# Score products on 64-column quarters of the TensorE array in a decoder layer

## The reference

```
x = layernorm(x + gelu(x @ (w1 @ w2.T * sparse_mask) + b2))
x = layernorm(x + cross_attention(x, ctx, wq, wk, wv, wo))   # 32 query heads, 8 key/value heads of 128, 64 context rows, rope
x = layernorm(x + x @ W.T + b + routed_lora(x))              # router softmax over 8 experts, rank 16
```

```
scores = jnp.einsum('bhqd,bhkd->bhqk', q, k) / scale
attn = jax.nn.softmax(scores + m[:, None, :, :], axis=-1)
out = jnp.einsum('bhqk,bhkd->bhqd', attn, v)
return out.transpose(0, 2, 1, 3).reshape(bs, sq, HQ * DV) @ wo
```

## Time and profile before

| | |
|---|---|
| median of 3 runs | 532.72 us (531.84 to 533.61) |
| profiled execution | 532.04 us, span 530.2 us, granted TensorE clock 0.994 |
| TensorE matmul busy | 507.9 us, 3149 records |
| score products (L350) | 1024 records, 32 blocks |
| VectorE, ScalarE, GpSimd busy | 408.9, 259.8, 269.0 us |

### The profile page before, as it was taken

The page is one execution under the profiler, slowest core; times in us unless marked ns, Lnnn a source line. Parts: engine busy times, 40 slices in busy tenths (PEclk is TensorE's granted clock), DMA queues, the critical chain, the costliest instruction groups (busy, mean ns, idle before and its releaser), DMA issues.

```text
span 530.2 us, 9033 instructions
## 1 busy us (share of the span) xinstructions
PE 507.9 (96%) x3149; PEld 419.4 (79%) x3149; DVE 408.9 (77%) x742; ACT 259.8 (49%) x462; POOL 269.0 (51%) x343
## 2 busy tenths in 40 slices
PE   5899999999999999999999999999999999969992
PEld 4677788888888888888888888888888888758781
DVE  3556888878878877787788788878887888999575
ACT  4372375753555355636563555354546544263332
POOL 2173255944575367527653854484547533136624
PEclk9999999999999999999999999999999999999997
DMA  8942010203020302020212023002200230000004
GB/s 302 356 129 90 1 41 0 77 4 121 0 81 0 119 0 79 22 96 0 79 56 63 0 79 108 11 0 79 79 0 5 76 61 1 2 0 1 1 2 158
DMA packets 27598, 31.51 MB, mean 59 GB/s; under 512 B 6321, under 2 KB 14769, under 8 KB 27578
## 3 DMA queue, kind: packets, MB, share of 16 engines
q1 hardware_dynamic: 27578, 31.25, 18.2%
HBM read 29.15 MB, written 2.10 MB: 59 GB/s over the span
## 4 chain that ended last, share of the span: by engine, by line
PE 90%; DVE 3%; DMA 2%; POOL 1%; SPq 1%; issue 1%; ACT 1%; DVEq 0%; POOLq 0%; ACTq 0%
PE bank L255 25%; PE bank L257 24%; PE bank L256 24%; PE bank L350 11%; PE bank L357 3%; PE bank L261 2%; DMA CTX<-in_ctx_dram 2%; DVE VWl L1105 1%; PE bank L300 1%; DVE BST L1155 1%; DVE X L1347 1%; PE bank L390 0%; PE bank L301 0%; ACT VWh L768 0%; SPq L203 0%
## 5 line engine op out<-in xcount | busy, mean ns | idle before, releaser
L1694 POOL TENSOR_TENSOR QS<-QS,SIN 128x512 f32<-128x512 f32 x64 | 82.7, 1292 | 98.9 <-ACT QS L768 93.7
L1105 DVE TENSOR_TENSOR VWl<-bank,VWh 64x512 fp32r<-64x512 f32 (+1 forms) x132 | 90.8, 688 | 20.3 <-ACT VWh L768 18.3
L255 PE MATMUL bank<-XTh,WQh 128*128 128x512 f32 x256 | 101.6, 397 | 0.0
L257 PE MATMUL bank<-XTh,WQl 128*128 128x512 f32 x256 | 99.9, 390 | 0.0
L256 PE MATMUL bank<-XTl,WQh 128*128 128x512 f32 x256 | 99.9, 390 | 0.0
L768 ACT ACTIVATE QS<-bank 128x512 f32<-128x512 f32 x64 | 38.3, 598 | 116.6 <-PE bank L257 116.3
L768 ACT ACTIVATE VWh<-bank 64x512 fp32r<-64x512 f32 (+1 forms) x132 | 78.2, 593 | 27.4 <-PE bank L257 24.2
L350 PEld LDWEIGHTS bank<-KK,QR 64*128 64x128 f32 x1024 | 59.6, 188 | 10.9 <-issue 10.8
L1219 DVE TENSOR_TENSOR bank<-bank,COS 128x512 f32<-128x512 f32 x64 | 44.6, 697 | 30.0 <-ACT QS L768 29.3
L350 PE MATMUL bank<-KK,QR 64*128 64x64 f32 x1024 | 64.1, 275 | 0.0
L1700 POOL TENSOR_TENSOR SM<-SM,RI 128x512 f32<-128x512 f32 x32 | 33.4, 1045 | 53.9 <-DVE RI L1265 53.8
(11 more groups left out here) (145 smaller groups left out, 955.8 us busy)
## 6 DMA issues: line engine op xcount, KB each, us to landing
WQr<-in_L_xattn_wq_dram SPq DMA_DIRECT2D x8, 1024.0 KB, 5.5
WOr<-in_L_xattn_wo_dram SPq DMA_DIRECT2D x8, 1024.0 KB, 5.5
KVr<-in_L_xattn_wk_dram SPq DMA_DIRECT2D x8, 256.0 KB, 5.3
KVr<-in_L_xattn_wv_dram SPq DMA_DIRECT2D x8, 256.0 KB, 5.6
out_dram<-X SPq DMA_DIRECT2D x8, 256.0 KB, 2.1
X<-in_x_dram SPq DMA_DIRECT2D x3, 512.0 KB, 10.0
WQr<-in_L_attn_w_dram SPq DMA_DIRECT2D x4, 256.0 KB, 3.1
WOr<-in_L_attn_w_dram SPq DMA_DIRECT2D x4, 256.0 KB, 4.9
```

Source lines behind the costliest of these rows:

```text
L255: pe.matmul(o, lh, rh, start=start, stop=False)
L257: return pe.matmul(o, ll, rh, start=False, stop=stop)
L1105: return dve.tensor_tensor(o, i, f32(hi), ALU.subtract)
L1694: pool.tensor_tensor(q, q, SIN[:, :].unsqueeze(1).broadcast_to([P, 2, S]), ALU.mult)\
```

## The change

Each score product of 64 rows by 128 tokens becomes two of 64 rows by 64 tokens. The first 64 tokens of a tile use columns 0 to 63 of the array and write bank partitions 0 to 63, the second 64 tokens columns 64 to 127 and partitions 64 to 127. With the two heads on the two row halves this makes four quarters. In program order stand: head 0 first half, head 1 first half, head 0 second half, head 1 second half, then the other rope half. The moving operand is unchanged. What is written, and where, is the same.

In front of each block TensorE increments a new semaphore, `s_begun`, which nobody waits for. All waits of the block go onto that instruction of the sequencer and the one before it; before, one of them stood on the block's first product. Lines behind 345 move down by up to three, so the products are L352 in the changed kernel.

```
         t_mm pt_hi pt_lo vw_mm vw_hi vw_lo pv_mm
         f_mm f_hi f_lo tile_sum mean_out lg_mm lg_step lg_exp r_out rt_mm rt_out tt_mm ts_out ts_hi ts_lo
-        fy_mm fy_out bias_in""".split()
+        fy_mm fy_out bias_in s_begun""".split()
...
                 if u == 0:
                     pe.wait_ge(sm["k_rot"], g + 1)
+                pe.sem_inc(sm["s_begun"], 1)
                 for t in range(4):
                     b = 2 * (u // 2) + t // TPB
                     for f in range(2):
-                        for a in range(2):
+                        for n in range(4):
+                            a, part = n % 2, slice(64 * (n // 2), 64 * (n // 2) + 64)
                             head = slice(64 * a, 64 * a + 64)
-                            m = pe.matmul(bank[:, S_BANK + a, t * KS:(t + 1) * KS], QR[head, u % 2, f, t * P:(t + 1) * P],
+                            m = pe.matmul(bank[part, S_BANK + a, t * KS:(t + 1) * KS],
+                                          QR[head, u % 2, f, t * P + part.start:t * P + part.stop],
                                           KK[head, b, f, :], start=f == 0, stop=f == 1)
                 m.then_inc(sm["s_mm"], 1)
```

## The result

The changed kernel takes 509.16 us, the median of four runs (508.37 to 510.26), against 533.16 us for four runs of the kernel before (531.84 to 533.61): ratio 0.9555, 95% interval 0.9527 to 0.9584, 24.0 us faster. The profiled execution took 509.79 us, its span 508.0, at a mean granted clock of 0.987. The forecast was 507.7.

What follows compares the result with a forecast made beforehand. TensorE was taken to bound the loop, busy 51.5 of 51.5 us a round. Savings of 31 x 0.86 = 26.7, minus 1.6 for late waits and 0.1 for the increment, gave -25.0 us: 507.7 from 532.72, range 504.5 to 535.5.

Steps and rivals of the forecast that it cites:

- The step: In a score block: four quarters work side by side, each load or matmul 54 + 4 ns, so 58 ns a step.
- The block: One score block: 16 x 0.058 + 0.14 = 1.07 us against 1.93, saving 0.86.
- Rival 1: In score blocks the two column halves of a row half take turns: no change or slower, up to 535.2 us; chance 0.33.
- Rivals 2 and 3: Feeding score blocks is the bound: a pair every 25 ns, 527.0 us, chance 0.12; or 40 ns, 557 us, chance 0.05.
- rival 2: In score blocks a pair starts only every 25 ns whatever its quarter: block 1.74 us, time 527.0; chance 0.12.
- Rival 4: In the head-group loop VectorE becomes the bound, needing 48.1 us a round where it has 40.9; no chance of its own.
- The increment: At the last score block the sequencer hands over products after the wait: 0 to 0.35 us once, taken as 0.1.
- the cover: At score block entries: a quarter microsecond per matmul queued ahead; without it 31 x 0.35 = 11 us at stake.
- Late waits: In the tail: the last block's 0.86 us lost, plus 1.6 us more waiting for VectorE's splits, bounds 0 and 4.8.
- Its sign: In the profile after: TensorE's waits still only at the start and tail, there a little longer.

Runs made afterwards that it cites:

- half_keys: Changed kernel with 32 of the 64 keys as moving columns, half the scores left out; 509.43 us, ratio 0.9545 to the kernel before.
- eighths: Changed kernel with products of 32 tokens on eight tiles, two row halves by four column quarters, all scores computed; 519.63 us, ratio 0.9722 to before.
- one_row_half: Changed kernel with all products on rows 0 to 63, so both heads share one row half; 538.12 us, ratio 1.0080 to the kernel before.
- eighths_half_keys: Changed kernel with products of 32 tokens on eight tiles and 32 of the 64 keys, half the scores left out; 514.32 us, one execution.
- inc_only: Kernel before plus only the s_begun increment ahead of each score block, all block waits on the sequencer; 533.37 us, ratio 1.0000.
- halves_first: Changed kernel with quarters reordered: both halves of head 0, then both of head 1; 508.54 us, ratio 0.9525 to the kernel before.
- one_column_half: Changed kernel with both token halves on columns 0 to 63, overwriting each other, token half outside rope half; 536.33 us, ratio 1.0048 to before.
- halves_outer: Changed kernel with the loop over column halves outside that over rope halves, all products computed; 509.66 us, ratio 0.9548 to the kernel before.

## Why the prediction was right

**The step.** The forecast took the four quarters as working side by side like the two halves, at 54 + 4 = 58 ns; the records say 58.3. half_keys shows that the load sets it, as the forecast had it for the block before; for the changed block it had put load and matmul at the same 58, and the run separates them: the matmul is a little shorter, 56 ns by the run eighths. The load was forecast at about 134 ns and is 135. The forecast's 54 + 4 are 53.4 + 5 by the steps, which changes nothing in the sum.

**The block.** Forecast 1.07 us and 0.86 saved, measured 1.09 and 0.84. The difference is in what stands beside the 16 steps, 0.16 instead of 0.14, and in the 58.3. Of the 0.16, 0.013 is new: four starts 6.5 ns apart take that much longer than two.

**Rival 1, column halves in turn.** It fell with the change's own profile, and one_row_half shows its mechanism wrong by itself: 2.06 us where turns make 3.7. The rule of the Trainium skill in TensorE: Matmul & The Clock Gate, Part 3 (The mechanism), that a load overlaps a running matmul only where the row groups differ, would have made this the result. In one_row_half all records have the same rows, and they overlap; the measurement decides against the "only". The Trainium skill in TensorEngine Tiling (Array Packing), Key Properties, says that tiles load and multiply independently, and the trace agrees, in 1.09 us for 64 pairs. (The forecast's 1.87 us for 32 records at 58 ns should be 1.86; nothing hangs on it.)

**Rivals 2 and 3, feeding.** Pairs start 6.5 ns apart on different quarters, so the spacing of the logits was a matter of one tile and not of issue. Their 22 ns is a mean over a first pair of loads 5 ns apart; their matmuls start 25 ns apart from the second on, which is the price that rival 2 took. The limit exists, and nearer than the block shows: some 8.3 ns a pair in eighths_half_keys against the 14.6 that the quarters need. Rival 2's mechanism comes into play with tiles of half the size, if at another price than its 25 ns.

**Rival 4, the loop becomes VectorE's.** It did not: the round is 48.1 us as forecast, and VectorE is busy 85% of the stretch from first to last block.

**The increment.** Forecast 0 to 0.35 us once, taken as 0.1. inc_only finds no difference, with an interval of 0.22% (1.2 us) either way: it can't tell 0.1 from none, and it does exclude the 11 us that the forecast saw at stake without the cover.

**Late waits.** Forecast: 1.6 us of longer waits in the tail and the last block's 0.86 lost. The blocks save 32 x 0.84 = 26.9 us; the stretch between first block and the matmul behind the last shows 24.87; so 2.0 us were given back. With the last block counted as the forecast did it is 31 x 0.84 = 26.0, less 1.2. The size was nearly right and the place mostly wrong, so that the 1.6 came out is luck. Before, the second and the third score block start at:

```profile
85.71 2.00 PE L350 MATMUL bank<-KK,QR 64*128 64x64 f32 x32
...
96.38 2.00 PE L350 MATMUL bank<-KK,QR 64*128 64x64 f32 x32
```

and after:

```profile
86.59 1.16 PE L352 MATMUL bank<-KK,QR 64*64 64x64 f32 x64
...
90.76 0.63 PE L360 MATMUL bank<-ID,SM 128*128 128x128 f32 x4
91.46 0.39 PE L255 MATMUL bank<-CTh,KVh 128*128 128x256 f32 x1
...
96.70 0.63 PE L360 MATMUL bank<-ID,SM 128*128 128x128 f32 x4
97.26 1.16 PE L352 MATMUL bank<-KK,QR 64*64 64x64 f32 x64
```

Both are 10.67 us apart, so the whole 0.84 of that block went into waits between them. By the distances of the starts they are three: 0.2 us in front of the transposes at 90.76 and again in front of those at 96.70, and 0.3 in front of the matmul at 91.46. The chain of waits of the kernel after has VectorE's rotation up to 91.42, in front of that matmul, and the timeline of GpSimd has the multiplication that the second transposes need, up to 96.55:

```profile
90.82 0.60 DVE QR L1232
...
95.51 1.04 POOL L1703 TENSOR_TENSOR SM<-SM,RI 128x512 f32<-128x512 f32 x1
```

The view of waits names none of the three: a matmul's record lasts longer than the distance to the next start, so a wait that is shorter than that overhang leaves little or no idle time. A further 0.2 went behind the first block, where TensorE waits for XTl:

```profile
78.97 1.16 PE L352 MATMUL bank<-KK,QR 64*64 64x64 f32 x64
80.29 0.47 PE L255 MATMUL bank<-XTh,WQh 128*128 128x512 f32 x1 [0.16 <-DVE XTl L1108]
```

That is 1.0 us in the prologue, which the forecast had not looked at, since its cover was read from a view of waits that names none between 77 and 458 us. Its sign that waits would be longer only at the start and in the tail did not hold there. The 28 distances behind them, up to the last block, give back 0.16 in all. In the tail 0.28 go before the last block and 0.55 of its own 0.84 behind it. The matmul behind the last block before, and the same place after:

```profile
461.24 0.47 PE L255 MATMUL bank<-VWh,PTh 128*128 128x512 f32 x1 [0.78 <-DVE PTl L1105]
...
434.72 0.66 PE L360 MATMUL bank<-ID,SM 128*128 128x128 f32 x4 [0.29 <-DVE X L1286]
435.41 1.16 PE L352 MATMUL bank<-KK,QR 64*64 64x64 f32 x64
437.91 0.47 PE L255 MATMUL bank<-VWh,PTh 128*128 128x512 f32 x1 [1.34 <-DVE PTl L1108]
```

So the last block kept 0.29, where the forecast gave it nothing, and the tail's VWl waits stayed at 4.0 us, where it had put a third more on the whole group.

**What the forecast left out: the granted clock.** The profiled executions differ by 22.2 us and not by 24.9. The windows of the kernel after (columns as in the earlier trace rows, the clock behind the POOL figures) show two stretches at half the clock. Each follows a wait of TensorE, 2.5 us for the context's DMA and 2.4 us for VWl:

```profile
16.00:18.00 2.00, 1.61 (x6) 1.51 (x7) 0.80 (x2) 1.09 (x2) 0.00 (x0) 0.61 1.06 388
...
450.00:453.00 3.00, 2.63 (x6) 2.04 (x7) 2.93 (x6) 1.52 (x2) 0.54 (x3) 0.50 0.00 0
```

0.50 is 1.2 GHz, 1.00 is 2.4. The timeline of the second:

```profile
450.37 0.79 PE L255 MATMUL bank<-VWh,PTh 128*128 128x512 f32 x1 [2.41 <-DVE VWl L1108]
450.96 0.63 PE L256 MATMUL bank<-VWl,PTh 128*128 128x512 f32 x1
451.38 0.63 PE L257 MATMUL bank<-VWh,PTl 128*128 128x512 f32 x1
```

and of the same place before:

```profile
473.70 0.50 PE L255 MATMUL bank<-VWh,PTh 128*128 128x512 f32 x1 [2.41 <-DVE VWl L1105]
474.04 0.40 PE L256 MATMUL bank<-VWl,PTh 128*128 128x512 f32 x1
474.28 0.40 PE L257 MATMUL bank<-VWh,PTl 128*128 128x512 f32 x1
```

Behind the same wait of 2.41 us the matmuls come 0.43 us apart in one execution and 0.23 in the other; six of them cost 1.2 us, the +1.13 of the table. The first stretch costs 1.6 us in the same way: from the context's transposes to the seventh matmul behind them it is 16.39 to 19.86 us, and 16.47 to 18.35 before. That is the +1.54, with some 0.07 the other way. Neither belongs to the change. Before the first score block all kernels run the same instructions, and that block starts at 77.14 in the profile of inc_only, 77.49 in half_keys, 78.57 in halves_first and 79.15 in one_column_half. Behind the VWl wait, 2.40 to 2.42 us in all ten profiles, the clock fell in six: with the change, and in one_column_half, half_keys, one_row_half, eighths and eighths_half_keys. It did not fall in the kernel before, inc_only, halves_first and halves_outer. So it falls with long blocks and with short ones. In one_row_half it fell 1.2 us behind the end of the wait at 479.46 and stood at 0.50 from 482 to 484 us.

Over the 12 runs of the kernel before in the second set, those at a mean clock of 0.994 took 531.7 to 532.1 us and those at 0.984 534.6 to 536.7. The profile on which the forecast stood was one at 0.994. With medians on both sides this mostly cancels: 533.16 - 509.16 = 24.0, 1.0 us less than forecast, which is inside this spread. (509.16 lies 1.5 us above the 507.7; the other 0.4 are the median before, 533.16 with a fourth run where the forecast had 532.72.)

## What to carry to other kernels

A matmul whose weight load is the longer side gains when its stationary operand is cut along columns onto column tiles that would stand idle, even for the same rows and in any order near by: here two tiles of 64 by 64 for one of 64 by 128 took a block from 1.93 to 1.09 us. Cut only until the load is as short as the matmul (58 against 56 ns a step here, so a further cut had next to nothing to gain) or until the pairs reach the rate at which they are fed, some 8 ns a pair here; eight tiles were slower than four (1.41 against 1.09 us). Before summing such a saving over all blocks, look at those in the prologue and the tail one by one, because there a neighbour's work is late at once, by the distances of the starts and not by the view of waits alone, and look at how far the profiled execution's clock lies from that of the median run.

## What the runs showed of the hardware

Five things I had not expected. Records on different quarters start 6.5 ns apart, where the matmuls of the logits, all on one tile, come 25 ns apart. A record goes ahead of others in program order that wait for another quarter, as halves_outer against one_column_half shows; eight records in a row on two quarters cost 0.05 us a block. A load keeps its full price when the matmul shrinks: loads of 32, 64 and 128 columns last 106, 135 and 188 ns, 0.83 to 0.91 ns a column, and 32 moving columns instead of 64 left the step at 58.3 ns. Once some 32 load and matmul pairs of a block are used up, further ones come every 8.3 ns (eighths_half_keys). And behind one and the same wait of 2.4 us the clock was granted at 2.4 GHz in some executions and at 1.2 GHz for 2.7 us in others.
